# Eight PSUM banks in one pool, half of one subtraction on GpSimd, and a new order of the work: a two-layer graph transformer on one core

## The reference, cut to what matters

```python
def layer0(x, adj):                      # x: 128 graphs x 128 nodes x 256 features, float32; adj: 0/1
    q, k, v = x@Wq+bq, x@Wk+bk, x@Wv+bv  # 8 heads of 32
    s = einsum('bnhd,bmhd->bhnm', q, k) / sqrt(32); s = where(adj == 0, -inf, s)
    y = einsum('bhnm,bmhd->bnhd', softmax(s), v).reshape(b, n, d) @ Wo + bo + x
    return (y - mean(y)) * rsqrt(var(y) + 1e-5) * gamma + beta
def layer1(x, adj):
    n1 = ln(x); q, k, v = n1@wq+bq, n1@wk+bk, n1@wv+bv
    s = q k^T / sqrt(32) + where(adj > 0, 0.1 * adj * adj, -inf)
    x1 = x + (softmax(s) v) @ wo + bo
    return x1 + gelu(ln(x1) @ w1 + b1) @ w2 + b2      # w1: 256x1024, w2: 1024x256
out = layer1(layer0(x, adj), adj)
```

## Time and profile before

| what | value |
| --- | --- |
| median of 3 runs | 2299.97 us |
| profiled execution | 2303.0 us, its span 2301.2 us |
| PE busy | 2200.5 us (96%) |
| DVE, ACT, POOL busy | 2034.2 (88%), 1838.3 (80%), 1300.8 (57%) |
| mean granted PE clock | 0.985 of full |
| DMA | 32 GB/s on average |

### The profile page before, as it was taken

One profiled execution on the slowest core, in us unless ns is written; L12 is line 12 of the kernel. 1 busy time (PEld: TensorE's weight loads), 2 busy tenths in 40 slices (PEclk: granted clock), 3 DMA queues, 4 the chain that ended last, 5 costly groups with the idle time before them and its releaser, 6 DMA issues.

```text
span 2301.2 us, 58678 instructions
## 1 busy us (share of the span) xinstructions
PE 2200.5 (96%) x19008; PEld 1906.3 (83%) x19008; DVE 2034.2 (88%) x7173; ACT 1838.3 (80%) x5774; POOL 1300.8 (57%) x909
## 2 busy tenths in 40 slices
PE   6789999999999999999999999999999999999987
PEld 5678888888888888888888888888888888888776
DVE  5799999999999999999999999999999999999862
ACT  4688889888888888888888888888888888888862
POOL 2566565566566566556566656556656556556530
PEclk7999999999999999999999999999999999999988
DMA  4101101101100101100101110101110110110000
GB/s 126 35 22 38 33 21 32 36 27 36 32 23 27 36 27 36 32 27 24 36 27 36 33 35 14 36 29 35 36 32 14 36 36 27 36 32 6 24 10 19
DMA packets 80766, 72.77 MB, mean 32 GB/s; under 512 B 3008, under 2 KB 72256, under 8 KB 80704
## 3 DMA queue, kind: packets, MB, share of 16 engines
q1 hardware_dynamic: 80704, 71.98, 10.3%
HBM read 55.20 MB, written 16.78 MB: 31 GB/s over the span
## 4 chain that ended last, share of the span: by engine, by line
PE 59%; DVE 19%; ACT 13%; issue 7%; POOL 1%; DVEq 0%; DMA 0%; ACTq 0%; SPq 0%; POOLq 0%
PE ps_j L413 39%; PE ps_s L374 8%; PE ps_t L389 6%; DVE hl L821 4%; ACT pm L532 4%; DVE r L813 4%; ACT hh L603 3%; PE ps_j L424 3%; DVE pm L717 3%; PE ps_o L405 3%; ACT hf L609 2%; DVE hf L766 2%; ACT L603 2%; DVE stats L798 2%; DVE q1l L762 1%
## 5 line engine op out<-in xcount | busy, mean ns | idle before, releaser
L870 POOL TENSOR_TENSOR pm<-pm,rinv 128x512 f32<-128x512 f32 x512 | 559.8, 1109 | 633.6 <-DVE rinv L728 633.6
L532 ACT ACTIVATE pm<-pm,nmax 128x128 f32<-128x128 f32 x2048 | 794.1, 391 | 120.1 <-DVE nmax L717 116.6
L717 DVE CUSTOM_DVE_ANT_0 pm<-ps_s,m 128x128 f32<-128x128 f32 x2048 | 458.5, 285 | 68.8 <-PE ps_s L374 62.0
L532 ACT ACTIVATION_READ_ACCUMULATOR pm<-pm,nmax 128x1 f32 x2048 | 386.0, 188 | 0.0
L821 DVE TENSOR_TENSOR hl<-hf,hh 128x512 fp32r<-128x512 f32 x256 | 282.5, 1131 | 34.1 <-ACT hf L609 31.3
L389 PE MATMUL ps_t<-ident,pm 128*128 128x128 f32 x2048 | 286.3, 278 | 17.1 <-POOL pm L870 16.6
L413 PE MATMUL ps_j<-w2h,hh 128*128 128x256 f32 x1024 | 294.8, 288 | 5.7 <-DVE hl L821 5.7
L413 PE MATMUL ps_j<-w2h,hl 128*128 128x256 f32 x1024 | 287.8, 281 | 0.0
L413 PE MATMUL ps_j<-w2l,hh 128*128 128x256 f32 x1024 | 287.8, 281 | 0.0
L389 PEld LDWEIGHTS ps_t<-ident,pm 128*128 128x128 f32 x2048 | 232.5, 142 | 45.4 <-POOL pm L870 21.6
L885 POOL TENSOR_TENSOR rstd<-veps,power 128x4 f32<-128x4 f32 x96 | 98.0, 1021 | 279.6 <-DVE veps L806 276.5
(11 more groups left out here) (148 smaller groups left out, 6370.4 us busy)
## 6 DMA issues: line engine op xcount, KB each, us to landing
xTr<-in_xT SPq DMA_DIRECT2D x32, 512.0 KB, 3.7
xy<-in_x SPq DMA_DIRECT2D x32, 512.0 KB, 3.9
out<-x SPq DMA_DIRECT2D x32, 512.0 KB, 2.9
m<-in_adj SPq DMA_DIRECT2D x32, 256.0 KB, 2.8
a<-in_adj SPq DMA_DIRECT2D x32, 256.0 KB, 4.2
r<-in_wo SPq DMA_DIRECT2D x2, 256.0 KB, 5.9
x<-in_w SPq DMA_DIRECT2D x1, 512.0 KB, 8.7
v<-in_w SPq DMA_DIRECT2D x1, 512.0 KB, 7.2
```

What stands on the lines that cost most here:

```text
L532: last = nc.scalar.activation(pm[:, g % 2, h, :], pm[:, g % 2, h, :], ACT.Exp, bias=nmax[:, g % 2, h:h + 1], scale=-1.0, accum_out=rsum[:, ...
L717: last = nc.vector.tensor_tensor_reduce(out=pm[:, g % 2, h, :], in0=ps_s[c][:, j * N:(j + 1) * N], in1=m[:, g, :], scale=1.0, scalar=3e38, ...
L870: tt(pm[:, g % 2, hs, :], pm[:, g % 2, hs, :], rinv[:, g % 2, hs].rearrange("p (h a) -> p h a", a=1).to_broadcast([P, HC, N]), ALU.mult).t ...
```

## The change

1. All eight PSUM banks are one pool. The table `JOBS` has 66 entries for an iteration and names the bank of each by hand; scores (`S0`, `S1`: graph and half), transposed probabilities (`F0`, `F1`) and outputs of `values` (`V0`, `V1`) are jobs like the others. A job waits for the job before it in the same bank. `masked`, `pt_a`, `pt_b`, `ot_lo` and the like are replaced by the two semaphores of each bank.
2. `split_h` is done by POOL for odd m, by DVE for even m, with a semaphore for each.
3. The bodies of PE, ACT, DVE and POOL are listed in another order. DVE also gets waits without work, `flipped`, for the end of certain transposes.
4. The bias products of the set-up use one bank, and two of their semaphore counts become one.

```diff
 JOBS = [
-    ("MLP2", 0, 3), ("QKV0", 4, 0), ("MLP2", 1, 3), ("QKV0", 5, 0), ("T1", 0, 1), ("WO1", 0, 2), ("T1", 1, 1),
...
-BANKS = 3
+    ("QKV0", 0, 0, 1), ("F1", 1, 2, 5), ("S1", 4, 2, 7), ("S1", 5, 2, 3), ("S1", 6, 2, 6), ("S1", 7, 2, 2),
+    ("QKV0", 1, 0, 0), ("QKV0", 2, 0, 5), ("MLP2", 0, 3, 1), ("F1", 2, 2, 7), ("QKV0", 3, 0, 4), ("F1", 3, 2, 0),
+    ("QKV0", 4, 0, 6), ("MLP2", 1, 3, 2), ("V1", 0, 2, 4), ("S0", 0, 0, 7), ("S0", 1, 0, 5), ("S0", 2, 0, 0),
...
+    ("MLP1", 0, 2, 2), ("MLP1", 1, 2, 1), ("MLP1", 2, 2, 6), ("MLP1", 3, 2, 7), ("MLP1", 4, 2, 0), ("MLP1", 5, 2, 2),
+    ("V0", 1, 0, 5), ("MLP1", 6, 2, 3), ("MLP1", 7, 2, 7), ("WO0", 0, 0, 6), ("WO0", 1, 0, 2), ("F1", 0, 1, 4),
+BANKS = 8
...
             def open_job(b, name, n):
                 pos = POS[name, n]
-                need(pe, job_free[pos % BANKS], uses_before(b + BEHIND[pos], pos))
-                return ps_j[pos % BANKS]
+                need(pe, job_free[BANK[pos]], uses_before(b + BEHIND[pos], pos))
+                return ps[BANK[pos]]
...
             def scores(l, b, g):
...
-                    before = earlier(l, b, g, 1)
-                    if before:
-                        pe.wait_ge(masked[before[0]], 2 * slot(*before[1:]) + 2)
+                    outs = [open_job(b, f"S{l}", 2 * g + c) for c in (0, 1)]
...
             def mlp_down(b, g):
                 if exists(b):
                     if g == 0:
-                        pe.wait_ge(h_lo, FC * (b + 1))
+                        pe.wait_ge(h_lo[0], FC // 2 * (b + 1))
+                        pe.wait_ge(h_lo[1], FC // 2 * (b + 1))
...
+            def flipped(l, b, g, c):
+                if exists(b):
+                    filled(dve, b, f"F{l}", 2 * g + c)
...
+            def split_h(b, m):
+                if exists(b):
+                    pool.wait_ge(h_hi, FC * b + m + 1)
+                    taken(pool, b, "MLP1", m)
+                    tt(hh[1][:, m, :], hf[:, m % 2, :], hh[0][:, m, :].bitcast(F32),
+                       ALU.subtract).then_inc(h_lo[1], 1)
...
+                pad_k(Y, i - 2, 3); normalise(X, i - 1, 2, 1); normalise(X, i - 1, 3, 0); normalise(X, i - 1, 3, 1)
+                add_b2(i - 3); add_bo0(i - 1); normalise(Y, i - 2, 0, 0); split_h(i - 3, 1); split_h(i - 3, 3)
+                normalise(Y, i - 2, 0, 1); split_h(i - 3, 5); split_h(i - 3, 7); add_bo1(i - 2); root(0, i - 1)
```

More of the change, by code:

```diff
@@ L47, in exists @@
     return 0 <= b < NB if isinstance(b, int) else True
[L50 to L53, removed]
+POS = {(name, n): at for at, (name, n, _, _) in enumerate(JOBS)}
+BEHIND = [job[2] for job in JOBS]
+BANK = [job[3] for job in JOBS]
 def uses_before(i, pos):
+    same = [q for q in range(len(JOBS)) if BANK[q] == BANK[pos]]
     def count(it):
-        same = range(pos % BANKS, len(JOBS), BANKS)
         n = sum(exists(k - BEHIND[q]) for k in range(FIRST, it) for q in same)
@@ L74, in slot @@
     return b * G + g
[L77 to L88, removed]
 def program(nc, x, xT, adj, w):
@@ L152, in program @@
         rstd = sb("rstd", [P, 3, G])
[L154 to L157, removed]
+        ps = [bank(f"ps{n}") for n in range(BANKS)]
         qkv_loaded = [sem(f"qkv_loaded{l}") for l in (0, 1)]
@@ L480, in body @@
             def body(i):
[L481 to L490, removed]
@@ L491, in body @@
-                mlp_up(i - 2, 4); mlp_up(i - 2, 5); mlp_up(i - 2, 6); mlp_up(i - 2, 7); out_proj(X, i, 0)
-                out_proj(X, i, 1); flip(Y, i - 1, 0, 0); flip(Y, i - 1, 0, 1); qkv(X, i + 1, 0); qkv(X, i + 1, 1)
-                qkv(X, i + 1, 2); scores(Y, i - 1, 2); qkv(X, i + 1, 3)
+                qkv(X, i, 0); flip(Y, i - 2, 0, 1); scores(Y, i - 2, 2); scores(Y, i - 2, 3); qkv(X, i, 1)
+                qkv(X, i, 2); mlp_down(i - 3, 0); flip(Y, i - 2, 1, 0); qkv(X, i, 3); flip(Y, i - 2, 1, 1)
@@ new lines, in body @@
+                qkv(X, i, 4); mlp_down(i - 3, 1); mlp_down(i - 3, 2); values(Y, i - 2, 0); scores(X, i, 0)
+                scores(X, i, 1); flip(Y, i - 2, 2, 0); flip(Y, i - 2, 2, 1); mlp_down(i - 3, 3); qkv(X, i, 5)
+                flip(Y, i - 2, 3, 0); flip(Y, i - 2, 3, 1); flip_rows("T1", i - 1, 0); flip_rows("T1", i - 1, 1)
+                out_proj(Y, i - 2, 0); values(Y, i - 2, 1); scores(X, i, 2); flip(X, i, 0, 0); flip(X, i, 0, 1)
+                qkv(Y, i - 1, 0); out_proj(Y, i - 2, 1); qkv(Y, i - 1, 1); qkv(Y, i - 1, 2); flip(X, i, 1, 0)
@@ new lines, in body @@
+                flip(X, i, 1, 1); qkv(Y, i - 1, 3); scores(X, i, 3); values(X, i, 0); qkv(Y, i - 1, 4)
+                qkv(Y, i - 1, 5); flip(X, i, 2, 0); flip_rows("T2", i - 2, 0); flip_rows("T2", i - 2, 1)
+                scores(Y, i - 1, 0); scores(Y, i - 1, 1); flip(X, i, 2, 1); flip(X, i, 3, 0); flip(X, i, 3, 1)
+                mlp_up(i - 2, 0); mlp_up(i - 2, 1); mlp_up(i - 2, 2); mlp_up(i - 2, 3); mlp_up(i - 2, 4)
+                mlp_up(i - 2, 5); values(X, i, 1); mlp_up(i - 2, 6); mlp_up(i - 2, 7); out_proj(X, i, 0)
@@ L495, in _ @@
+                out_proj(X, i, 1); flip(Y, i - 1, 0, 0)
             iterate(pe, body, {FIRST: first_weights})
@@ new lines, in body @@
+                x_lo(i, 1); residual("WO0", i - 1, 0); split_h(i - 3, 6); residual("WO0", i - 1, 1)
+                norm_stats(0, i - 1); copy_pt(Y, i - 2, 0); qk_lo(X, i, 0); mask_scores(Y, i - 2, 2, 0)
+                recip(Y, i - 2, 1); norm_rows(0, i - 1); qk_lo(X, i, 1); mask_scores(Y, i - 2, 2, 1)
+                flipped(Y, i - 2, 1, 0); mask_scores(Y, i - 2, 3, 0); qk_lo(X, i, 2); flipped(Y, i - 2, 1, 1)
+                mask_scores(Y, i - 2, 3, 1); copy_pt(Y, i - 2, 1); v_out(X, i, 0); qk_lo(X, i, 3); mask1(i - 1)
```

182 lines of the change are left out of this document (86 added, 96 removed), and 10 rows, old and new, of the table JOBS.

## The result

The changed kernel takes 2285.4 us (median of 4 runs, 2283.5 to 2286.5) against 2300.4 of the kernel before on the same chip: a ratio of 0.9934, 95% interval 0.9917 to 0.9951, so 11 to 19 us faster. The forecast was 24 us faster with a range that holds it.

The account below looks back on a forecast made before the run. TensorE was taken as the bound, busy 67.49 of 68.65 us a batch. Terms -1.2 - 0.45 + 0.9 = -0.75 us, 32 times, -24 us: 2276 us against 2299.97; range 2224 to 2316, the forecast's own 2262 to 2292.

Parts of the forecast that it names:

- Borders: TensorE's switches between scores, values and full-size products fall from 21 to 15 a batch, 0.2 us each: 1.2 us saved.
- The bound from the other side: Two scores in succession on TensorE cost a border at each joint, which leaves 0.6 us a batch saved.
- Out_proj: TensorE's wait at out_proj(X, i, 0) for gelu to empty its bank goes with the new bank: -0.45 us a batch.
- Transposes: TensorE's wait for norm_rows(2) before the MLP's transposes grows by 0.9 us a batch, bounds -1.1 to +1.5.
- split_h, nothing: Odd split_h on GpSimd, 1.3 us each, relieve VectorE, which isn't the bound: no direct gain, nothing counted before mlp_down.
- The root rival: GpSimd's root of the first norm comes late behind split_h and add_bo1, delaying qkv(X, i, 4): 2305 to 2350, chance 0.22.
- the relief was used up: Even split_h on VectorE held by odd ones on GpSimd, up to 5.2 us; transposes' wait then at its upper bound.
- Other waits: VectorE's mask held by flipped(Y, 2, 0) up to 1.3 us, but covered: nothing; set-up waits under 1 us per run.
- The shorter wait at the transposes: Rival: the wait for norm_rows(2) doesn't grow (2247) or goes (2212); put at 2235, chance 0.24.
- The relief of VectorE: Argument for the shorter-wait rival: VectorE has 3 to 7 us less work a batch.

Follow-up runs that it names:

- m_apart: a_mix with layer 0's graph 1 scores listed behind the two half flips of layer 1, two borders more: 2275.8 us, ratio 0.9893.
- a_split_dve: The changed kernel with all eight split_h on VectorE, none on GpSimd: 2282.9 us, ratio 0.9920.
- b_split_pool: The kernel before with the odd split_h moved to GpSimd, nothing else changed: 2289.4 us, ratio 0.9951.
- a_hold: The changed kernel with one added wait: GpSimd's normalise(X, 2, 1) waits until norm_rows(2) on VectorE has ended: 2252.1 us, ratio 0.9792.
- m_split_dve: a_mix with all eight split_h on VectorE: 2242.7 us, ratio 0.9742.
- a_first: The changed kernel with norm_rows(2) listed on VectorE before the last qk_lo of layer 1: 2249.0 us, ratio 0.9772.
- a_mix: a_hold with recip(X, 2) before copy_pt(X, 1) and layer 1's last qk_lo between graph 3's two mask halves: 2244.0 us, ratio 0.9754.
- a_late: The changed kernel with v_out(Y, 0) before norm_rows(2) on VectorE: 2286.4 us, ratio 0.9934.

## Why the prediction was right, and what it missed

- *Borders, -1.2 us a batch.* Right: a joint of scores is free in the rows after, and a border costs 0.2 in m_apart, where no wait behind it takes it up. The bound from the other side, a border for each joint, is excluded. What remains of the period when the other terms are taken off is 1.3 (see the sum).
- *Out_proj, -0.45.* The wait went. The reason given, the bank, is one of two that suffice (a_split_dve, b_split_pool).
- *Transposes, +0.9.* Measured +0.92. Both parts named are there, 0.4 less cover and a third row held by `normalise`, but the second was worked out only in part: the row costs 0.72 (a_hold), and 0.27 comes back because the first row no longer meets a `pad_k`, which the prediction did not have. The 0.5 forecast for the two was the middle between two bounds, so that it came so near 0.45 is in part luck. That TensorE's scores and not VectorE's load set the start of the chain was right: the rows of the norm start 3.53 us after the scores' first matmul, before (1047.67 - 1044.14) and after (1042.95 - 1039.43) alike.
- *split_h, nothing.* Right in both kernels that could tell (a_split_dve and m_split_dve, with all of it on VectorE, stand within their intervals). The root rival did not come about: `norm_rows(0)` started at 1072.73, 2.05 us after the root did, behind other work of VectorE, and `qkv(X, i, 4)` followed its flip without a wait. Nor did the two engines hold each other so long that the relief was used up: the even `split_h` took 0.69 us at the median and 1.48 at most.
- *Other waits.* Two small ones were not forecast, and nearly cancel: the second half flip of graph 2 of layer 1 now waits for `normalise` (+0.28), and the second half of the transposes for the MLP no longer starts late (0.22 us behind the last transpose of the first half before, 0.11 after; with the slower start that follows a wait, -0.17).
- *Sum.* -0.73 against -0.75 a period: -1.3 for the borders, -0.45, +0.92, +0.28 and -0.17. What was missed is a term that the forecast did not have: the longer wait lets the granted clock fall in some batches, 7 x 1.54 = 10.8 us. Without these stretches the change would stand at some 2275, against 2276 forecast. That this is so near is luck too. In the profiled executions the first 28 periods give 20 us without the stretches, and what lies behind them, the last three batches, gives 8 where the forecast's rate gives some 2. That no such stretch was in the loop before, with a wait of 1.1 us, was visible in the profile, where the clock is full from slice to slice; a wait twice as long asked for that row to be looked at.
- *Rivals.* The shorter wait at the transposes (2247 with the wait as it was) came about only by a_hold, a_first and a_mix, at 2252, 2249 and 2244. The relief of VectorE did not bring it.

What stays open: which of the waits at the transposes are followed by the lower clock. In the loop, waits of 1.3 us and less never were, in nine kernels (before and all runs but a_split_dve and a_late), waits of 2.0 us were in 7 of 26 batches in each of two kernels, waits of 2.24 in 2 of 26. Chance alone is not a good answer: in the changed kernel all 26 waits are alike to 0.01 us, and the long periods stand almost evenly, 1, 5, 4, 5, 4 and 5 periods apart; in a_late the three are 13 and 14 apart. What picks them no run shows.

## What to carry to other kernels

Where one engine's instruction can hold another's, the order on the engine that isn't the bound matters at the one place where the bound waits: a wait added to GpSimd for 0.7 us of quiet gave 22 us, and 11 more by the clock. A move that gathers work of one form saves its borders only where no wait stands behind them, and the gathered work may have been the cover of another engine, so the price has to be read at the place. And a wait that grows can cost more than its length, once the clock answers to it (2.02 us did, in seven batches), though not in proportion (2.24 us did so less often).

## What the runs showed of the hardware that was not expected

In the loop, the granted clock fell to the lower level behind some waits of 2.0 to 2.2 us and behind none of 1.3 us or less, in a TensorE that was 97% busy over the period (65.99 of 67.92 us), and a longer wait did not bring it more often.

A small VectorE instruction with SBUF tiles on both sides, 0.40 us alone, took 1.99 and 1.12 us beside GpSimd instructions of 2.00 and 1.08, each until the GpSimd instruction had ended. Between the two rows GpSimd's next instruction came in, so the group of four was held twice.

The changed kernel also loads instructions all through the loop. The pages of before and after, queue by queue (packets, MB, share):

```profile
q14 instruction: 28, 0.23, 0.0%
```

```profile
q14 instruction: 153, 1.25, 0.2%
```

Five packets come in each period, where before had none from 401 to 2085 us. The count is the same with `split_h` on either engine (153 in a_split_dve, 27 in b_split_pool). No wait of TensorE is put down to them, and the period agreed with the forecast without them.
